# Attention on one Trainium2 core: order of cap, normalisation and rope within a sequence's slot

## The reference

```python
x = x + 0.5 * _L0_ffn_ref(_layernorm(x), ...)
x = x + _L0_attn_ref(_layernorm(x), Wq, Wk, Wv, Wo)
x = x + 0.5 * _L0_ffn_ref(_layernorm(x), ...)
```

```python
q = (X @ Wq)...; k = (X @ Wk)...; v = (X @ Wv)...
q = q * cos + _rotate_half(q) * sin
k = k * cos + _rotate_half(k) * sin
att = jnp.einsum('bhqd,bhkd->bhqk', q, k) * scale
att = SOFTCAP * jnp.tanh(att / SOFTCAP)
att = jnp.where(causal[None, None], att, -jnp.inf)
att = jax.nn.softmax(att, axis=-1)
y = jnp.einsum('bhqk,bhkd->bhqd', att, v)
return y.transpose(0, 2, 1, 3).reshape(b, t, NH * HD) @ Wo
```

## Time and profile before

| | |
|---|---|
| median of 3 runs | 1034.19 us (1033.8 to 1035.34) |
| the profiled execution, its own time | 1035.26 us |
| its span, first to last instruction | 1033.5 us |
| mean granted TensorE clock | 0.971 |
| busy over the span: PE, DVE, ACT, POOL | 929.0, 688.1, 535.4, 487.1 us |
| matmuls L80 to L82 in attention, one of 128x256 | 0.28 to 0.31 us |

### The profile page before, as it was taken

One profiled execution on the slowest core, in us unless ns is written; L12 is line 12 of the kernel. 1 busy time (PEld: TensorE's weight loads), 2 busy tenths in 40 slices (PEclk: granted clock), 3 DMA queues, 4 the chain that ended last, 5 costly groups with the idle time before them and its releaser, 6 DMA issues. The chain is left out here.

```text
span 1033.5 us, 18341 instructions
## 1 busy us (share of the span) xinstructions
PE 929.0 (90%) x6274; PEld 699.1 (68%) x6274; DVE 688.1 (67%) x1702; ACT 535.4 (52%) x798; POOL 487.1 (47%) x534
## 2 busy tenths in 40 slices
PE   2999998999999489989999998966999989999998
PEld 1788876777778456555656565635888867777787
DVE  4888767544444457888887788755888777453435
ACT  3666642132233167787778787753766532232322
POOL 5333203556541085777676677623422223655540
PEclk9999999999999699999999999986999999999999
DMA  5324225677773400001000100012143255777735
GB/s 185 117 90 128 69 82 162 169 183 182 180 168 97 142 1 22 21 21 41 21 21 20 39 12 11 18 55 87 55 129 109 69 162 127 179 186 178 176 64 168
DMA packets 95433, 101.91 MB, mean 99 GB/s; under 512 B 18688, under 2 KB 86656, under 8 KB 95360
## 3 DMA queue, kind: packets, MB, share of 16 engines
q1 hardware_dynamic: 83072, 83.17, 26.3%
q0 software_dynamic: 12288, 17.83, 10.1%
HBM read 65.44 MB, written 35.54 MB: 98 GB/s over the span
## 5 line engine op out<-in xcount | busy, mean ns | idle before, releaser
L80 PE MATMUL gu<-x_hi,gu_hi 128*128 128x512 f32 x308 | 139.5, 453 | 4.8 <-DVE act_gu L1124 4.8
L82 PE MATMUL gu<-x_lo,gu_hi 128*128 128x512 f32 x308 | 122.3, 397 | 0.0
L81 PE MATMUL gu<-x_hi,gu_lo 128*128 128x512 f32 x308 | 121.9, 396 | 0.0
L671 POOL DMA_INDIRECT rows<-z_rows,slots x64 | 68.1, 1063 | 75.7 <-DVE slots L1115 56.7
L957 ACT CAST a_hi<-act_gu 128x512 fp32r<-128x512 f32 x96 | 59.1, 616 | 84.0 <-DVE act_gu L1124 60.6
L1563 ACT ACTIVATE capped_at<-scores_at 128x2048 f32<-128x2048 f32 x64 | 93.0, 1454 | 15.4 <-PE scores_at L1450 15.4
L1647 POOL TENSOR_SCALAR_AFFINE_SELECT probs_at<-probs_at 128x1024 f32<-128x1024 f32 x64 | 76.1, 1189 | 50.2 <-ACT probs_at L1571 50.2
L1571 ACT ACTIVATE probs_at<-capped_at 128x2048 f32<-128x2048 f32 x64 | 95.1, 1487 | 3.0
L80 PE MATMUL down<-down_hi,a_hi 128*128 128x256 f32 x300 | 94.3, 314 | 0.2 <-DVE a_lo L1134 0.2
L1005 ACT ACTIVATE y<-gu,rows 128x256 f32<-128x256 f32 x64 | 30.3, 473 | 109.9 <-PE gu L887 76.9
L258 POOL TENSOR_TENSOR rstd_f<-var_in_f,neg_half 128x8 f32<-128x8 f32 x16 | 26.7, 1668 | 127.6 <-DVE var_in_f L253 127.6
(11 more groups left out here) (231 smaller groups left out, 2575.5 us busy)
## 6 DMA issues: line engine op xcount, KB each, us to landing
w_gu<-in_w_gate SPq DMA_DIRECT2D x64, 176.0 KB
w_gu<-in_w_up SPq DMA_DIRECT2D x64, 176.0 KB
w_down<-in_w_down SPq DMA_DIRECT2D x64, 176.0 KB
z_rows<-z SPq DMA_DIRECT2D x16, 512.0 KB, 3.1
acc<-base SPq DMA_DIRECT2D x10, 512.0 KB, 3.5
out<-base SPq DMA_DIRECT2D x10, 512.0 KB, 3.6
x_f<-in_X SPq DMA_DIRECT2D x8, 512.0 KB, 4.5
xn_at<-acc SPq DMA_DIRECT2D x16, 256.0 KB, 2.7
```

Of the source, the lines that this page charges most:

```text
L80: nc.tensor.matmul(out, w_hi, x_hi, start=first, stop=False)
L81: nc.tensor.matmul(out, w_lo, x_hi, start=False, stop=False)
L82: return nc.tensor.matmul(out, w_hi, x_lo, start=False, stop=last)
L671: pool.indirect_dma_start(out=gathered_rows[:, n, :], out_offset=None, in_=m.z_rows, in_offset=bass.IndirectOffsetOnAxis(ap=slots[:, e:e + ...
```

## The change

Four places in the attention stage, in the code of three engines. On ScalarE the third cap moves ahead of the second `y_hi_part`, and `normalise` moves from the slot's end to behind the second exponential. On GpSimd `rope` is cut into `rope_sin` and `rope_sum`; the sum of piece 0 goes behind the second mask. On TensorE `output` waits at first only for the low part of group 0, and for that of group 1 ahead of the first matmul that reads it. No instruction of computation is added or taken away.

```diff
             def output(b):
                 pe.wait_ge(o_lo_ready, 1)
-                pe.wait_ge(y_lo_ready, b * GROUPS + GROUPS)
+                pe.wait_ge(y_lo_ready, b * GROUPS + 1)
...
                 for t in range(QT):
                     for g in range(GROUPS):
+                        if t == 0 and g == 1:
+                            pe.wait_ge(y_lo_ready, b * GROUPS + GROUPS)
...
                 cap(b, 1)
                 exponential(b, 1)
+                if further:
+                    normalise(b + 2, held)
+                cap(b, 2)
                 if behind:
                     y_hi_part(b - 1, 1)
-                cap(b, 2)
                 exponential(b, 2)
...
                 if further:
-                    normalise(b + 2, held)
                     aT_hi_part(b + 2)
...
-            def rope(b, q, n):
+            def rope_sin(b, n):
                 pool.wait_ge(turned_ready, b * PIECES + n + 1)
                 at_least(pool, scores_ready, UNITS * (b - 1))
-                c = 2 * ((n - 1) % PIECES)
                 sin = m.sin[:].unsqueeze(1).to_broadcast([P, 2, SEQ])
                 pool.tensor_tensor(by_sin[:, n], turned[:, n], sin, ALU.mult).then_inc(sin_done, 1)
+
+            def rope_sum(b, q, n):
+                c = 2 * ((n - 1) % PIECES)
                 pool.wait_ge(sin_done, b * PIECES + n + 1)
                 pool.tensor_tensor(roped[:, q, c:c + 2, :], by_cos[:, n], by_sin[:, n], ALU.add).then_inc(roped_ready, 1)
...
                 causal(b, 0)
                 if ahead:
-                    rope(b + 1, 1 - q, 0)
+                    rope_sin(b + 1, 0)
                 causal(b, 1)
                 if ahead:
-                    rope(b + 1, 1 - q, 1)
+                    rope_sum(b + 1, 1 - q, 0)
+                    rope_sin(b + 1, 1)
+                    rope_sum(b + 1, 1 - q, 1)
                 causal(b, 2)
                 causal(b, 3)
```

More of the change, by code:

```diff
@@ L1662, in slot_of @@
                 if ahead:
-                    rope(b + 1, 1 - q, 2)
+                    rope_sin(b + 1, 2)
+                    rope_sum(b + 1, 1 - q, 2)
             zero = pool.to_reg(0.0)
@@ L1668, in _ @@
             for n in range(PIECES):
-                rope(0, 0, n)
+                rope_sin(0, n)
+                rope_sum(0, 0, n)
             slot_of(0, 0)
```

## The result

The changed kernel takes 1003.98 us (median of 4 runs, 1002.11 to 1004.58) against 1033.99 us before: a ratio of 0.9705, with a 95% interval of 0.9688 to 0.9722, so 30 us or 2.95% less. 1017 was forecast, with a range of 1007 to 1028: the direction was right, but the 17 us forecast are only a little over half of the 30 measured.

A forecast was written before the change was run, and what follows sets the result against it. TensorE bounds the stage, next the GpSimd-VectorE ring. Twelve slots 13.2 us, first gap 1.6, last two slots 0.8 and 1.9: 17.5 off the profiled 1035.3 gives 1017.8, which lies 1.1 above the median's scale, hence 1017 (1007 to 1028).

The forecast's parts named there:

- Third cap first: ScalarE's queue: third cap done at 540.9 instead of 543.67, so TensorE's wait ahead of the fourth scores goes.
- Split wait: TensorE's output: six first-group matmuls, some 0.75 us, go ahead of the wait for the second group's low part and cover it.
- TensorE's floor: Attention slot: 18.3 us if nothing else came late for TensorE, against 20.5 before.
- The clock: Three lower-clock stretches behind TensorE's gaps: 3.6 us between all gone and all kept; taken as gone.
- The ring of GpSimd and VectorE: Attention slot: a closed chain of the two engines' instructions, walked step by step, sets the pace at 19.4 us.
- The blocks: GpSimd and VectorE: with both VectorE inputs in SBUF, the second instruction stands for the other's whole instruction; rows show 1.78, 2.29 us.
- merely shared bandwidth: GpSimd and VectorE: if they only shared bandwidth, without an exclusive lock, the slot would be 18.3 us, the time some 1003.
- the length of the ring, the term 19.4 us: Slot: 13.3 us GpSimd work, 2.8 blocked, 3.3 from last sum to variance; saves 1.1 us a slot, 13.2 in twelve.
- rival A: Attention slot: collisions fall on VectorE's slack, slot 18.3 us, time 1003, or some 1010 with half gone; chance 0.15 for 1003 to 1012.
- the end of the stage: Two last slots: split saves about 0.8 us, last gap gives 1.9 of 2.33; clock there two us either way.
- B, the knot: Second low part blocked behind GpSimd's second sum: TensorE stands 1.75 us mid-output, slot 21.2, time 1038; 0.09 in full, 0.14 partly.
- C: Gap returns as TensorE waits, including for the third turned piece: slot 20.6 to 20.8 us, time 1031 to 1035; chance 0.07.

The follow-up runs named there:

- e1: The kernel before with only the third cap moved ahead of the second `y_hi_part`: 1014.57 us, ratio 0.9803.
- e4: The changed kernel with the normalisation back at the slot's end: 1004.79 us, ratio 0.9725.
- e2: The changed kernel with the output waiting for both low parts at once: 1015.23 us, ratio 0.9816.
- e3: The changed kernel with the first rope in one piece again, ahead of the second mask: 1005.46 us, ratio 0.9716.
- e7: The changed kernel with each rope sum over half of its columns, so GpSimd has less work and attention is partly left out: 1001.48 us, ratio 0.9676.
- e8: The kernel before with six more matmuls on TensorE in the gap ahead of the fourth scores, slots 1 to 13: 1029.90 us, ratio 0.9961.
- e6: The changed kernel with one more GpSimd instruction a slot, behind the fourth mask: 1012.54 us, ratio 0.9794.
- e5: The changed kernel with GpSimd's root moved behind the first mask: 1006.93 us, ratio 0.9737.
- e9: The changed kernel with VectorE's statistics moved from the slot's head to behind `aT_lo`, ahead of the quotient: 1001.33 us, ratio 0.9687.

## Why the prediction missed its range

What held, by its steps. *Third cap first*: the fourth scores wait no more, and e1 alone gives 20 of the 30 us. *Normalisation*: no price, and e4 finds no gain either; without it, TensorE's transposes come 0.24 us later in every second slot, and its wait for the first mask is 0.26 us shorter there. *Split wait*: 0.5 us a slot by e2, as worked out. *Rope split*: given no gain; 0.05 us a slot by e3, and perhaps 2 us in the whole stage. *TensorE's floor*: 18.3 forecast, 18.28 in e7. *The clock*: the low stretches are gone with the gap, but by e8's slots the three were worth 2.5 us rather than the 3.6 that bounded them. *The ring of GpSimd and VectorE*: it exists and it is closed, by e6 and e5. *The blocks*: as told; in the changed kernel the first low part takes 1.77 us while the sine product beside it keeps its 1.28, and the addition takes 2.32. So the time near 1003 does not speak for the merely shared bandwidth to which the prediction gave that figure.

What failed is **the length of the ring, the term 19.4 us**; it is 18.62. Against the slot from 550.47, in us after the transposes:

| step of the walk | forecast | measured |
|---|---|---|
| last sum ends | 2.65 | 2.5 |
| variance | 5.9 | 5.45 |
| first mask ends | 8.3 | 7.8 |
| second mask ends | 11.2 | 10.6 |
| quotient ends | 13.05 | 12.4 |
| second low part ends | 14.95 | 14.2 |
| addition ends | 17.3 | 16.5 |
| third sine product ends | 20.75 | 19.8 |
| third sum ends | 22.05 | 21.2 |

The order of the steps, who is blocked and by whom, came as the walk had them; nearly every link was charged a little too much. 0.3 us arose ahead of the variance: the walk started from one slot, whose statistics held a pause of 0.2 us that a regular slot doesn't have, and added the shift of the last sum in full. Another 0.4 us arose between the variance and the end, over some twelve handovers: I took the listed end of each instruction as the start of the one that it blocks, but the rows overlap. In the changed kernel the quotient is listed from 561.78 to 562.86, and the sine product that it held up, 1.27 us alone, ends at 564.01, so it ran from 562.74, 0.12 us ahead of the listed end. The first low part (558.32) and the addition (564.61), reckoned in the same way, ran from 0.11 and 0.13 us ahead of the listed ends of what had held them up. In every second slot the first low part wins its tie with the sine product; the walk put those slots at 19.5, and they too take 18.6.

The twelve slots gave 22.3 us where 13.2 were forecast: 9.1 us of the 13 missed. This step was also decisive for the choice between the cases: at 18.6 the ring and TensorE's floor with its small waits are 0.3 us apart, and the time comes within a microsecond of rival A's, though A's reason (no ring) is wrong. The other part is the end of the stage: 2.7 us forecast from the two last slots, 6.9 measured. There 0.8 and 1.9 us were put on waits alone, and the rows give 1.4 and 1.8; but in the kernel before the last slot's fourth scores and output ran at the lower clock and in the changed one they do not. They are the earlier trace rows's second row and what stands behind it: from these scores to the denominators behind the output, 24 matmuls long, it was 6.56 us before and is 3.70 after, so 2.9 us (the row of the denominators before, then the rows of scores and denominators after):

```profile
690.25 0.64 PE L1480 MATMUL den_at<-probs_at,ones_f 128*32 128x256 f32 x8
...
653.77 0.71 PE L1450 MATMUL scores_at<-roped_at 32*128 32x256 f32 x8 [0.50 <-ACT capped_at L1565]
...
657.47 0.64 PE L1480 MATMUL den_at<-probs_at,ones_f 128*32 128x256 f32 x8
```

I had allowed two us either way for the clock there and put nothing into the sum. Another 0.9 us lie behind that output; their cause is open.

The rivals. B, the knot: not in the changed kernel, whose second low part starts at 564.02, 0.07 us ahead of the sum at 564.09, the margin of the walk. In the slots of the other kind the second low part is held up, by the second sine product: from 544.98 it takes 1.15 us instead of 0.67:

```profile
544.98 1.15 DVE L1741 TENSOR_TENSOR y_lo_at<-y_at,y_hi_at 128x512 fp32r<-128x512 f32 x1
```

It ends at 546.13, 0.2 us before the seventh matmul of the output reads it, and costs nothing; e5 shows what it costs when it comes later. C: the waits for the turned piece at the output's start are 0.1 us a slot. The range failed since its lower bound was drawn through half of case A, while the ring's links had been read from rows of one slot to a tenth of a microsecond each and some fourteen of them added up. An error of 0.05 us a link was enough, since nearly all lay in one direction.

## What to carry to other kernels

An in-order engine that waits for a late input with a ready, wanted instruction right behind it is the first thing to look for: exchanging the two gave 20 of 30 us. When such a wait goes, walk once around the chain that comes next, but measure links from start to start in the rows, not from their listed durations, and let the uncertainty of the sum grow with their number. And when a ring of two engines sets the pace, reordering inside it may only move the wait, as in e5; take out of it what doesn't need to be there, as e9 does with the statistics.

## What the runs showed of the hardware

In the kernel before, eight gaps of 1.8 us or more stand ahead of the fourth scores. Three of the seven in the slots 1 to 13 were followed by a stretch at the lower clock (1.1 to 1.2 us more busy time for the same 16 listed matmuls each time, of which 0.6 to 1 us came out in the slot), and so was the last slot's of 2.33. The same gap of 2.33 us in e8 was not, nor was any of the gaps of 0.96 us there. Filling a part of each of the thirteen gaps with useless matmuls (1.87 us became 0.96) made the twelve slots 2.5 us shorter in all.

A `tensor_scalar` of 128x256 elements with one input took GpSimd 0.85 us (e6), three quarters of what a mask of 128x1024 takes (1.10).

VectorE's instructions with both inputs in SBUF and GpSimd's instructions that read SBUF ran one after the other in these rows, each as a whole block: the addition of 1.21 us is listed with 2.32, and the pair of masks behind it, 1.1 us each, with 3.27.
